# Routing products spread over TensorE's work, the routing chain moved behind the first inner blocks, and one step of the count blocks moved forward

## The chip, the cores and the metric

One Trainium2 chip, one NeuronCore of it. The metric is the device time of one execution in microseconds (us), the median over several runs. Engines: TensorE (PE), its weight loads (PEld), VectorE (DVE), ScalarE (ACT), GpSimd (POOL), SyncE (SP), which issues the transfers.

## What is computed

A graph network on 3125 nodes of 128 features and 100000 edges, in four blocks, each with a layer norm before it and a residual around it. Two of them matter here.

Block 0 is a gated recurrent network of four layers:

```python
for l in range(NUM_LAYERS):            # 4
    m = x @ weight[l]
    agg = segment_sum(m[src], dst)
    x = gru_cell(agg, x, ...)          # reset, update and new gates, x = (1-z)*n + z*x
```

Block 3 is a mixture of experts of three layers, with hidden size 256, four weak and four strong experts:

```python
for l in range(L):                     # 3
    agg = segment_sum(h[src], dst) / deg
    logits = concat([h, agg]) @ router_W[l] + router_b[l]
    gates = softmax of the two largest logits, zero elsewhere
    weak = relu(agg @ weak_W[l] + weak_b[l])                    # 4 experts
    strong = relu(agg @ strong_W1[l] + b1[l]) @ strong_W2[l] + b2[l]   # 4 experts, inner size 512
    h = h + sigmoid(h @ conf_W[l] + conf_b[l]) * sum_e gates[e] * expert[e]
```

Blocks 1 and 2 (two plain graph convolutions, and one with eight relation types) are not touched.

## The kernel before, in words

**Data.** The edges are turned once into a dense matrix of counts `A`, kept in SBUF in fp8; a segment sum is then a product of the node features with `A`. Nodes lie in 25 tiles of 128 (the last of 53), and the tiles in 7 chunks of 4, 4, 3, 4, 3, 4, 3 tiles, so of 512, 512, 384, 512, 384, 512 and 309 columns. A float32 value is carried as two float16 halves, so each sum takes two products per tile and most others three. PSUM has 8 banks, `bank[0]` to `bank[7]`. Every engine has its own list of instructions, written out by hand, and engines are tied by semaphores.

**The expert block** (`block_experts`, from 1635 us to 3197 us of the span). Per layer, the weights come in ten pieces, and ScalarE (`split_high`, L2317) and VectorE (`split_low`, L2170) turn each into two float16 halves in turn. Four of the pieces are split ahead of the first chunk; six (the fifth is `w1` of expert 2, then the two pieces of weak weights, then three more) are split inside the first chunk, behind `hidden(0, 0)`. Per chunk `ci`, TensorE does:

- `route` (L2431): per tile, products with the router's weights in float32, 9 columns wide, into bank 2. VectorE's `route` then adds the bias (L2193, `e_logits`) and runs a chain of small operations that ends in a wait for ScalarE's exponential (L2343) and in the gates (L2233).
- `hidden(ci, e, blocks)` (L2446): the inner blocks of strong expert `e`, 6 products each, into banks 4 and 5 in turn. Block x waits until ScalarE has taken block x-2 out of its bank (`s_kept`, L2353). VectorE then splits each block into halves (L2249, L2251).
- `edges(ci + 1, ...)` (L2407): the segment sum of the next chunk, in pieces between the rest: bank 0 (`KB - 1` = 1 of 2 halves of the features) behind `hidden(ci, 0)`, bank 1 in four pieces.
- `weak` (L2482): products of the weak experts of one tile; needs their weight pieces.
- `strong(ci, e)` (L2465): per tile, 12 products into bank 6 or 7; VectorE empties it (L2260, L2263). The last one, `strong(ci, 3)`, comes behind `turn(ci + 1)` (L2419), the transposes of the next chunk's nodes, and ahead of `route(ci + 1)`.

In VectorE's and in ScalarE's list `route(ci)` stands ahead of `hidden(ci, 0)`. So ScalarE's exponential, which needs VectorE's chain, is queued ahead of its relu of the first inner block.

**The gated block** (`block_gru`). Layer 0 has its segment sums ready from before, so its chunks hold little beside the gates' products. Per chunk TensorE does `gate_b` (L1051), a few tiles of layer 1's first sum, one step of `sym`, `gate_c` (L1063), `finish` of the chunk before (transposes L832 into bank `BT` = 7), and another step of `sym`. `sym` (class `Symmetric`) adds the matrix of packed counts to its transpose for block 2, in 169 steps of up to four transposes (L929) into bank 6 or 7 in turn, by the parity of the step's number, with one VectorE addition each (L948). Two conditions tie it to bank 7:

```python
n, b0, g = STEPS[self.pe_at]
k, bk = n % R, 6 + self.pe_at % 2
...
def other(bk):
    if bk == BT and made["turned"]:
        pe.wait_ge(g_low, made["turned"])
```

`g_low` comes from VectorE (L1299, in layer 3 L1295) once it has read what `finish` put into bank 7. In layer 0 there are two steps per chunk from chunk 1 on, 12 in all. In layers 1 to 3 there are eight steps per chunk, ahead of the tiles that `AMONG` names with "S" (1, 4, 6, 9, 13, 16, 19, 22), and `finish` comes behind the last tile of a chunk, or at tiles 18 and 22 of the next layer's first chunk. VectorE's list has the same steps at the same places (`dve_step`).

## Time and profile before

| what | value |
|---|---|
| median of 3 runs | 3232.41 us (3229.61 to 3233.78) |
| the profiled execution | 3232.69 us, span 3230.8 us |
| mean granted TensorE clock | 0.971 of full speed |
| TensorE busy | 2968.3 us, 92% of the span |
| VectorE busy | 2186.6 us, 68% |
| ScalarE busy | 909.9 us, 28% |

The span runs from the first to the last instruction. A wait is listed by the engine that sat idle and by what ended the idle time. A timeline lists instructions of the same line in one row where they follow each other. Matmuls overlap, so the duration of a row is a little longer than the distance to the start of the next row; the sums of the prediction go by distances between starts.

### The profile page before, as it was taken

How to read it: one execution, taken by the hardware profiler on the slowest of the kernel's cores; microseconds unless marked ns; L12 is line 12 of the kernel's file. 1: busy time of each engine (PE TensorE's matmuls, PEld its weight loads, DVE VectorE, ACT ScalarE, POOL GpSimd, SP SyncE). 2: the span in 40 equal slices, each digit the busy share in tenths (PEclk: the TensorE clock that was granted, in tenths of full speed). 3: DMA queues.
4: the chain of work that ended last, by engine and by line, in shares of the span. 5: the costliest groups of instructions: out<-in, count | busy, mean ns of one | idle time of the engine just before them, and what ended most of it. 6: DMA issues, size and time to landing. Idle time of an engine off the chain costs nothing. (4 is left out here: it accounts for less than half of the span.)

```text
span 3230.8 us, 47504 instructions
## 1 busy us (share of the span) xinstructions
PE 2968.3 (92%) x18761; PEld 1785.9 (55%) x18761; DVE 2186.6 (68%) x4024; ACT 909.9 (28%) x1695; POOL 16.8 (1%) x23
## 2 busy tenths in 40 slices
PE   2888889999988999999989999989999998999997
PEld 2566446656443545454545665655656664656665
DVE  7999555557227777776657666676666686666676
ACT  3888422124101000000032222233222233222222
POOL 2000000000000000000000000000000000000000
PEclk8999889999999999999989999999999999999999
DMA  5455347765006555544330000020000011000001
GB/s 127 144 155 149 95 151 231 229 222 185 22 6 187 157 169 154 178 142 131 83 105 3 4 3 4 3 82 4 6 4 4 3 33 53 3 4 3 4 3 42
DMA packets 310958, 265.84 MB, mean 82 GB/s; under 512 B 32767, under 2 KB 289409, under 8 KB 308174
## 3 DMA queue, kind: packets, MB, share of 16 engines
q1 hardware_dynamic: 296558, 259.28, 26.3%
q10 hardware_dynamic: 13760, 2.61, 0.4%
q8 instruction: 153, 2.51, 0.3%
q0 software_dynamic: 416, 0.85, 0.1%
q14 instruction: 71, 0.58, 0.1%
HBM read 172.67 MB, written 90.05 MB: 81 GB/s over the span
## 5 line engine op out<-in xcount | busy, mean ns | idle before, releaser
L1871 PE MATMUL psum<-r_wd,r_h 128*128 128x512 fp8e4 (+1 forms) x2600 | 567.1, 374 | 14.0 <-ACT r_h L229 13.6
L2446 PE MATMUL psum<-m_agg,m_weights 128*128 128x512 f16 (+2 forms) x2016 | 422.6, 362 | 33.3 <-ACT m_agg L2353 33.3
L2465 PE MATMUL psum<-m_weights,x_nodes 128*128 128x256 f16 (+1 forms) x3600 | 413.0, 273 | 17.0 <-DVE m_wtmp L2260 15.3
L2407 PE MATMUL psum<-counts,m_h 128*128 128x512 fp8e4 (+2 forms) x2100 | 416.0, 355 | 12.6 <-DVE m_h L2150 12.6
L1871 PEld LDWEIGHTS psum<-r_wd,r_h 128*128 128x128 f16 x2600 | 240.6, 96 | 307.8 <-issue 15.5
L2465 PEld LDWEIGHTS psum<-m_weights,x_nodes 128*128 128x128 f16 (+1 forms) x3600 | 350.3, 98 | 74.4 <-DVE m_wtmp L2260 22.0
L2446 PEld LDWEIGHTS psum<-m_agg,m_weights 128*128 128x128 f16 x2016 | 197.3, 101 | 241.2 <-issue 48.6
L2407 PEld LDWEIGHTS psum<-counts,m_h 128*128 128x128 f16 x2100 | 206.3, 98 | 209.1 <-issue 19.5
L2365 ACT ACTIVATE m_hT<-m_hT,m_g 128x256 f32<-128x256 f32 x300 | 135.3, 500 | 599.4 <-DVE m_hT L2274 599.4
L2353 ACT ACTIVATE m_agg<-psum,x_nodes 128x512 f32<-128x512 f32 (+2 forms) x336 | 236.2, 716 | 144.1 <-PE psum L2446 114.9
L2274 DVE SCALAR_TENSOR_TENSOR m_hT<-psum,x_nodes,m_bias 128x512 f32<-128x512 f32 (+1 forms) x150 | 112.0, 750 | 170.0 <-PE psum L2482 169.8
L2260 DVE SCALAR_TENSOR_TENSOR m_wtmp<-psum,x_nodes,m_bias 128x256 f32<-128x256 f32 (+1 forms) x300 | 144.9, 483 | 119.8 <-PE psum L2465 116.8
L2251 DVE TENSOR_TENSOR x_nodes<-m_agg,x_nodes 128x512 f16<-128x512 f32 (+2 forms) x336 | 209.8, 624 | 11.6
L2482 PE MATMUL psum<-m_weights,m_agg 128*128 128x512 f16 x900 | 206.5, 379 | 0.0
L754 PE MATMUL psum<-oh_c,oh_s 128*128 128x150 f16 x1566 | 156.2, 237 | 48.3 <-ACT counts L789 31.4
L948 DVE TENSOR_TENSOR sym_blocks<-sym_blocks,psum 128x1024 uint16<-128x1024 uint16 (+1 forms) x169 | 110.9, 665 | 96.6 <-PE psum L929 95.0
L754 PEld LDWEIGHTS psum<-oh_c,oh_s 128*128 128x128 f16 x1566 | 112.4, 100 | 111.4 <-issue 68.3
L788 ACT ACTIVATE strip<-psum 128x600 uint16<-128x600 f32 x239 | 162.5, 680 | 35.5 <-PE psum L754 33.7
L1076 PE MATMUL psum<-counts,g_h16b 128*128 128x512 fp8e4 (+2 forms) x700 | 158.4, 357 | 2.7 <-DVE g_h16b L1299 2.7
L2263 DVE SCALAR_TENSOR_TENSOR m_h<-m_wtmp,m_g,m_h 128x256 f32<-128x256 f32 (+1 forms) x300 | 145.3, 484 | 10.7
L2249 DVE CAST x_nodes<-m_agg 128x512 f16<-128x512 f32 (+2 forms) x336 | 131.2, 390 | 17.5 <-ACT m_agg L2353 7.7
L1966 DVE SCALAR_TENSOR_TENSOR x_nodes<-psum,r_dg,x_nodes 128x128 f32<-128x128 f32 (+1 forms) x200 | 70.1, 350 | 106.0 <-PE psum L1823 100.6
(312 smaller groups left out, 3367.2 us busy)
## 6 DMA issues: line engine op xcount, KB each, us to landing
r_wd<-packed_sym SPq DMA_DIRECT2D x120, 640.0 KB, 4.2
packed_counts<-strip SPq DMA_DIRECT2D x21, 1800.0 KB, 7.8
sym_blocks<-packed_counts SPq DMA_DIRECT2D x88, 384.0 KB, 4.5
packed_sym<-sym_blocks SPq DMA_DIRECT2D x84, 384.0 KB, 3.1
w_stage<-in_L_gnn_strong_W SPq DMA_DIRECT2D x12, 1024.0 KB, 6.5
m_weights<-in_L_gnn_strong_W SPq DMA_DIRECT2D x21, 512.0 KB, 4.9
x_parked<-x_nodes SPq DMA_DIRECT2D x2, 1600.0 KB, 5.9
x_nodes<-x_parked SPq DMA_DIRECT2D x2, 1600.0 KB, 6.3
```

The lines of the kernel that those rows point to most:

```text
L754: m = pe.matmul(psum[:, unit_at(u, w):unit_at(u, w) + UC], oh_s[q][:, k, :, v], oh_c[q][:, k, :, v], start=True, stop=True)
L788: act.activation(typed_home, typed, ACT.Copy, scale=0.5).then_inc(kept_a, 1)
L1076: m = pe.matmul(bank[bk][:, 0:cw], h16[l % 2][:, part, i, :], A[:, i, c_:c_ + cw], start=(i == 0 and part == 0), stop=(i == NT - 1 and par ...
L1871: m = pe.matmul(bank[pair[b]][:, 0:2 * cw], h16[:, part, p0 + i, :], f_[:, 2 * b:2 * b + 2, :], start=(p0 + i == 0 and part == 0), stop=(p ...
L2251: vec.tensor_tensor(s_[:, BANK:BANK + cw], wide32, s_[:, 0:cw], ALU.subtract).then_inc(s_split, 1)
L2260: vec.scalar_tensor_tensor(tmp[k % 2][0:r_, :], bank[6 + k % 2][0:r_, 0:H], k_strong[0:r_], bcast[0:r_, ge * H:(ge + 1) * H], ALU.mult, AL ...
L2263: vec.scalar_tensor_tensor(h2[0:r_, i, :], tmp[k % 2][0:r_, :], gates[ci % 2][0:r_, k, ge:ge + 1], h2[0:r_, i, :], ALU.mult, ALU.add).then ...
L2353: act.activation(agg[:, hh % 2, 0:cw], bank[4 + hh % 2][:, 0:cw], ACT.Relu, bias=b1s[:, e * FB + f:e * FB + f + 1], scale=k_hidden).then_i ...
L2407: m = pe.matmul(bank[kb][:, 0:cw], h16[:, part, i, kb * P:(kb + 1) * P], A[:, i, c_:c_ + cw], start=(i == 0 and part == 0), stop=(i == NT ...
L2446: m = pe.matmul(bank[4 + hh % 2][:, 0:cw], w_[:, i, kb, f * P:(f + 1) * P], agg16[:, j, kb, 0:cw], start=(x_ == 0), stop=(x_ == len(todo) ...
L2465: m = pe.matmul(bank[b_][0:r_, 0:H], s_[:, pa[0] * BANK + k * P:pa[0] * BANK + k * P + r_], w_[:, pa[1], f, :], start=(f == 0 and pa == PA ...
L2482: m = pe.matmul(bank[2 + pr % 2][0:r_, :], agg16[:, pa[0], kb, k * P:k * P + r_], w_[:, pa[1], kb, :], start=(y_ == 0), stop=(y_ == len(to ...
```

## The change

Three things are done.

1. In the gated block, one step of `sym` is put behind the last segment sum ahead of layer 0's chunk 1, on TensorE and on VectorE. The number of steps stays 169.
2. On TensorE, the routing products of chunk `ci + 1` are issued tile by tile among the tiles of `strong(ci, 3)`: the first behind its second tile. Those of the first chunk of a layer are issued among the first 12 tiles of `edges(1, [0])`, three tiles and one routing tile in turn, so that 13 tiles of that sum are left behind `hidden(0, 0)`.
3. On VectorE, the bias addition (`logits`) stays ahead of `hidden(ci, 0)`, and the rest of the chain (`route`) goes behind it, as does ScalarE's exponential. In the last chunk both stay ahead.

```diff
--- before.py
+++ after.py
@@ -1123,6 +1123,8 @@
                 pe.wait_ge(gate_high, 1)
                 pe.wait_ge(steps.handle, mark["gate_low"])
                 sum_chunk(0, EARLY + 1, gates_of=0)
+
+                sym.pe_step(other)
                 for ci in range(1, NCH):
                     gate_b(0, ci)
                     for i, _ in tiles_of(CH[ci - 2]) if ci >= 2 else ():
@@ -1352,6 +1354,7 @@
                     if ci == 0:
                         state(0, ci)
                         gate_a(0, EARLY + 1)
+                        sym.dve_step()
                     else:
                         finish(0, ci - 1)
                         sym.dve_step()
@@ -2183,15 +2186,19 @@
                         vec.scalar_tensor_tensor(agg16[:, 1, :, 0:cw], agg[:, :, 0:cw], sc[:, 1:2], agg16[:, 0, :, 0:cw], ALU.mult,
                                                  ALU.subtract).then_inc(e_mean_low, 1)
 
+                    def logits(ci):
+                        n = l * NCH + ci
+                        R_, _, n_ = chunk_rows(CH[ci])
+                        vec.wait_ge(mrw_in, MRW_IN)
+                        vec.wait_ge(e_routed, n + 1)
+                        vec.tensor_tensor(lg[0:R_, 0:n_, :], bank[2][0:R_, 0:n_ * (NE + 1)].rearrange("p (t e) -> p t e", e=NE + 1),
+                                          rb[0:R_, l, None, :].to_broadcast([R_, n_, NE + 1]), ALU.add).then_inc(e_logits, 1)
+
                     def route(ci):
                         n = l * NCH + ci
                         R_, _, n_ = chunk_rows(CH[ci])
+                        l_ = lg[0:R_, 0:n_, 0:NE]
                         vec.wait_ge(prio_made, 1)
-                        vec.wait_ge(mrw_in, MRW_IN)
-                        vec.wait_ge(e_routed, n + 1)
-                        l_ = lg[0:R_, 0:n_, 0:NE]
-                        vec.tensor_tensor(lg[0:R_, 0:n_, :], bank[2][0:R_, 0:n_ * (NE + 1)].rearrange("p (t e) -> p t e", e=NE + 1),
-                                          rb[0:R_, l, None, :].to_broadcast([R_, n_, NE + 1]), ALU.add).then_inc(e_logits, 1)
                         vec.wait_ge(e_logits, n + 1)
                         o1, o2, l2, e_ = (t_[0:R_, 0:n_, :] for t_ in rt)
                         S1 = [sm[0:R_, i_, 0:n_] for i_ in range(10)]
@@ -2285,8 +2292,12 @@
                     for ci in range(NCH):
                         more = ci + 1 < NCH
                         ts = tiles_of(CH[ci])
-                        route(ci)
+                        logits(ci)
+                        if not more:
+                            route(ci)
                         hidden(ci, 0, range(FB))
+                        if more:
+                            route(ci)
                         if ci == 0:
                             for k in range(FIRST, NPC):
                                 split_low(k)
@@ -2371,8 +2382,12 @@
                     act.wait_ge(steps.handle, mark["h_bias", l])
                     for ci in range(NCH):
                         ts = tiles_of(CH[ci])
-                        route(ci)
+
+                        if ci == NCH - 1:
+                            route(ci)
                         hidden(ci, 0, range(FB))
+                        if ci < NCH - 1:
+                            route(ci)
                         if ci == 0:
                             for k in range(FIRST, NPC):
                                 split_high(k)
@@ -2419,18 +2434,21 @@
                                 m = pe.transpose(bank[2 + kb][:, k * P:(k + 1) * P], h2[:, i, kb * P:(kb + 1) * P], ident[:])
                             m.then_inc(h_turned, 1)
 
-                    def route(ci):
+                    def route_tile(ci, k):
+
                         n = l * NCH + ci
-                        pe.wait_ge(e_mean, KB * (n + 1))
-                        pe.wait_ge(h_kept, KB * (n + 1))
-                        pe.wait_ge(mrw_in, MRW_IN)
-                        for i, k in tiles_of(CH[ci]):
-                            r_ = rows_of(i)
-                            for kk in range(2 * KB):
-                                lhs = (hT if kk < KB else agg)[:, kk % KB, k * P:k * P + r_]
-                                m = pe.matmul(bank[2][0:r_, k * (NE + 1):(k + 1) * (NE + 1)], lhs, rw[:, l, kk, :],
-                                              start=(kk == 0), stop=(kk == 2 * KB - 1))
-                        m.then_inc(e_routed, 1)
+                        ts = tiles_of(CH[ci])
+                        r_ = rows_of(ts[k][0])
+                        if k == 0:
+                            pe.wait_ge(e_mean, KB * (n + 1))
+                            pe.wait_ge(h_kept, KB * (n + 1))
+                            pe.wait_ge(mrw_in, MRW_IN)
+                        for kk in range(2 * KB):
+                            lhs = (hT if kk < KB else agg)[:, kk % KB, k * P:k * P + r_]
+                            m = pe.matmul(bank[2][0:r_, k * (NE + 1):(k + 1) * (NE + 1)], lhs, rw[:, l, kk, :],
+                                          start=(kk == 0), stop=(kk == 2 * KB - 1))
+                        if k == len(ts) - 1:
+                            m.then_inc(e_routed, 1)
 
                     def hidden(ci, e, blocks):
                         cw = CH[ci][1]
@@ -2447,10 +2465,10 @@
                                               start=(x_ == 0), stop=(x_ == len(todo) - 1))
                             m.then_inc(s_hidden, 1)
 
-                    def strong(ci, e):
+                    def strong(ci, e, tiles=None):
                         w_ = pair_of(PNO[("w2", e)], FB)
                         pe.wait_ge(w_low, l * NPC + PNO[("w2", e)] + 1)
-                        for i, k in tiles_of(CH[ci]):
+                        for i, k in tiles_of(CH[ci]) if tiles is None else tiles:
                             r_ = rows_of(i)
                             b_ = 6 + k % 2
                             if b_ in freed_at:
@@ -2485,13 +2503,17 @@
 
                     edges(0)
                     turn(0)
+                    ROUTE_IN = 12
+                    per = ROUTE_IN // len(tiles_of(CH[0]))
+                    for i, k in tiles_of(CH[0]):
+                        edges(1, [0], range(k * per, (k + 1) * per))
+                        route_tile(0, k)
                     for ci in range(NCH):
                         more = ci + 1 < NCH
                         ts = tiles_of(CH[ci])
-                        route(ci)
                         hidden(ci, 0, range(FB))
                         if more:
-                            edges(ci + 1, range(KB - 1))
+                            edges(ci + 1, range(KB - 1), range(0 if ci else ROUTE_IN, NT))
                         weak(ci, ts[0:1])
                         for e in range(1, NSG):
                             hidden(ci, e, range(HALF))
@@ -2503,7 +2525,13 @@
                         if more:
                             edges(ci + 1, [KB - 1], CUTS_E[-1])
                             turn(ci + 1)
-                        strong(ci, NSG - 1)
+                            next_ = len(tiles_of(CH[ci + 1]))
+                            for k in range(max(len(ts), next_ + 1)):
+                                strong(ci, NSG - 1, ts[k:k + 1])
+                                if 0 < k <= next_:
+                                    route_tile(ci + 1, k - 1)
+                        else:
+                            strong(ci, NSG - 1)
 
                 for l in range(NLAY):
                     dve_layer(l)
```

## Rows read from the trace of the kernel before

**Rows 1.** The page, busy time of the engines (share of the span) and instructions.

```profile
PE 2968.3 (92%) x18761; PEld 1785.9 (55%) x18761; DVE 2186.6 (68%) x4024; ACT 909.9 (28%) x1695; POOL 16.8 (1%) x23
```

**Rows 2.** TensorE's waits, 1680 to 3200 us: us in total, times, longest.

```profile
PE psum L2446 <- ACT m_agg L2353: 32.3, 32, 2.1
PE psum L2465 <- DVE m_wtmp L2260: 15.3, 21, 1.4
```

**Rows 3.** Timeline of TensorE, expert layer 0: start us, us, engine, line [idle before].

```profile
1748.09 2.79 PE L2465 MATMUL psum<-m_weights,x_nodes 128*128 128x256 f16 x24 [0.87 <-DVE m_wtmp L2260]
...
1754.21 2.75 PE L2446 MATMUL psum<-m_agg,m_weights 128*128 128x512 f16 x12
1758.39 2.76 PE L2446 MATMUL psum<-m_agg,m_weights 128*128 128x512 f16 x12 [1.43 <-ACT m_agg L2353]
1760.99 8.29 PE L2407 MATMUL psum<-counts,m_h 128*128 128x384 fp8e4 x50
...
1832.01 2.12 PE L2446 MATMUL psum<-m_agg,m_weights 128*128 128x384 f16 x12 [1.86 <-ACT m_agg L2353]
```

**Rows 4.** Timeline of all engines, expert layer 1, its first chunk.

```profile
2185.02 1.04 PE L2419 MATMUL psum<-ident,m_h 128*128 128x128 f32 x8
...
2191.27 7.81 PE L2446 MATMUL psum<-m_agg,m_weights 128*128 128x512 f16 x24
2191.55 0.20 DVE L2193 TENSOR_TENSOR x_nodes<-psum,m_rb 128x36 f32<-128x36 f32 x1 [2.46 <-PE psum L2431]
...
2194.57 0.21 ACT L2343 ACTIVATE x_nodes<-x_nodes 128x8 f32<-128x8 f32 x1 [6.80 <-DVE x_nodes L2219]
...
2195.98 0.19 DVE L2233 TENSOR_TENSOR m_g<-m_rt,m_rt 128x32 f32<-128x32 f32 x1
...
2198.91 10.96 PE L2407 MATMUL psum<-counts,m_h 128*128 128x512 fp8e4 x50
...
2200.39 0.69 DVE L2251 TENSOR_TENSOR x_nodes<-m_agg,x_nodes 128x512 f16<-128x512 f32 x1
...
2201.00 1.28 DVE L2170 SCALAR_TENSOR_TENSOR m_weights<-m_weights,m_wmax 128x1024 f16<-128x1024 f32 x1
...
2209.71 2.75 PE L2482 MATMUL psum<-m_weights,m_agg 128*128 128x512 f16 x12
...
2213.80 1.28 DVE L2170 SCALAR_TENSOR_TENSOR m_weights<-x_nodes,m_wmax,m_weights 128x1024 f16<-128x1024 f32 x1 [1.28 <-ACT m_weights L2317]
...
2220.97 2.79 PE L2465 MATMUL psum<-m_weights,x_nodes 128*128 128x256 f16 x24 [1.14 <-DVE m_wtmp L2260]
```

**Rows 5.** Timeline of TensorE, start of expert layer 1.

```profile
2161.38 23.80 PE L2407 MATMUL psum<-counts,m_h 128*128 128x512 fp8e4 x100 [4.20 <-DVE m_h L2150]
```

**Rows 6.** Waits, all engines, gated layer 0, 377 to 450 us.

```profile
PE psum L929 <- DVE g_h16b L1299: 19.4, 6, 3.4
```

**Rows 7.** Timeline of all engines, gated layer 0.

```profile
404.93 0.75 DVE L1270 SCALAR_TENSOR_TENSOR g_t<-psum,g_sc,g_r 128x512 f32<-128x512 f32 x1 [0.77 <-ACT g_r L1170]
...
408.13 0.56 DVE L1299 SCALAR_TENSOR_TENSOR g_h16b<-psum,g_h16b 128x384 f16<-128x384 f32 x1 [1.74 <-ACT g_h16b L1184]
...
408.84 1.09 PE L929 MATMUL psum<-ident,sym_blocks 128*128 128x128 f32 x4 [3.14 <-DVE g_h16b L1299]
...
410.57 0.69 DVE L1280 TENSOR_TENSOR g_t<-g_ht,g_n 128x512 f32<-128x512 f32 x1
...
412.62 0.69 DVE L1262 SCALAR_TENSOR_TENSOR g_hn<-g_ht,g_hn 128x512 f16<-128x512 f32 x1
...
416.69 0.62 DVE L1270 SCALAR_TENSOR_TENSOR g_t<-psum,g_sc,g_r 128x384 f32<-128x384 f32 x1 [0.50 <-ACT g_r L1170]
```

**Rows 8.** Timeline, gated layer 1 (two rows) and gated layer 3.

```profile
483.22 0.60 PE L929 MATMUL psum<-ident,sym_blocks 128*128 128x128 f32 x4
...
483.69 0.69 DVE L1299 SCALAR_TENSOR_TENSOR g_h<-psum,g_h 128x512 f16<-128x512 f32 x1 [1.47 <-ACT g_h L1184]
...
729.71 0.69 DVE L1295 TENSOR_TENSOR x_nodes<-x_nodes,psum 128x512 f32<-128x512 f32 x1 [0.77 <-PE psum L832]
```

## The prediction

> **What bounds the kernel now.** I read the page first: TensorE is busy for 92% of the span [rows 1], so the kernel gets faster only where TensorE idles or runs at its lower clock. The waits come next, by stage. In the expert block TensorE loses 32.3 us to ScalarE's relu of inner blocks and 15.3 us to VectorE's emptying of the strong experts' banks [rows 2]. The timeline shows where [rows 3]. Behind the routing products two inner blocks run, TensorE then idles for 1.43 us (512 columns) or 1.86 us (384), and two more follow. The reason is ScalarE's order: the exponential stands ahead of the relu, and it comes 3.0 us after VectorE's bias addition (L2193 to L2343) [rows 4]. The other loss is 0.87 us ahead of the third tile of the last strong expert [rows 3].
>
> In gated layer 0 the waits show six stops of TensorE, 19.4 us together, at a count step [rows 6]. That is the step behind `finish`: it writes bank 7, and VectorE must first have read the transposes there. The timeline shows one of 3.14 us, and a chunk takes 11.76 us from one L1270 to the next [rows 7].
>
> **Part 1, routing chain behind the inner blocks, chunks 1 to 5.** Each layer has three such chunks of 512 columns and two of 384. For 512, the four blocks took 1760.99 - 1754.21 = 6.78 us; twice the second pair (1760.99 - 1758.39 = 2.60) is 5.20, so 1.58 us go. For 384 I take the idle time and 0.14 us for the pipeline's refill, 2.0 us. Sum 9 x 1.58 + 6 x 2.0 = 26.2 us. What could come next: the second pair then waits for the relu alone, which is shorter than the two blocks between, and the split by VectorE (about 1.1 us per block) keeps up with a block of 1.30 us. VectorE ends its splits 2.17 us after TensorE's last inner block (2198.91 to 2201.08) [rows 4]; then come the chain and the gates (2195.98 + 0.19 - 2191.75 = 4.4 us), so the gates are there 6.6 us after the blocks. TensorE has the next chunk's sum there, 50 products, 10.80 us for 512 columns [rows 4] and 8.29 for 384 [rows 3], before the weak products. So the chain is hidden in chunks 1 to 5. The last chunk keeps its order and its waits.
>
> **Part 2, routing products between strong tiles.** One routing tile costs 0.87 us (1748.09 to 1754.21 is 6.12 us, less 2.63 us for two strong tiles, over four). It is the same work elsewhere; what it brings is that it fills the 0.87 us ahead of the third tile. Of the 15.3 us, I leave some 3.8 us (three first chunks, 1.14 in the row shown [rows 4]) and 2.0 us (last chunks), and take 9.5 us. The end of the products, and so `e_routed`, stays where it is.
>
> **Part 3, the first chunk of each layer.** Here the move speaks against the change, because the six weight splits stand behind the chain on both engines. In layer 1 [rows 4]: the transposes end at 2185.02 + 0.88 = 2185.9. With 24 products of the sum (5.2 us, 0.216 each) and 3.5 us of routing, routing ends at 2194.6 instead of 2191.3; inner blocks end at 2199.8, VectorE's splits at 2202.0, the gates at 2206.4. The first of the six splits then starts at 2206.4 instead of 2201.0, the last ends at 2220.5 instead of 2215.1 (2.56 us each). TensorE finished the rest of the sum at 2199.8 + 26 x 0.216 = 2205.4 and needs the second split for its weak products: it stands from 2205.4 to about 2210. It then stops again at the third tile of the first strong expert, which VectorE releases 5.9 us after its last split (2215.1 to 2220.97), so at 2226.4. That point moves by +5.4 us, though TensorE had 4.3 us less to do before it. Three layers: +16.2 us. The idle time of 0.79 us ahead of routing and the slow routing products there lie before that point and bring nothing.
>
> What the stops do to the clock: the stop of 4.20 us at the layer's start was followed by 100 products in 23.80 us [rows 5], where 100 at full clock take 21.6. A stop of about this size comes right before the point above. I take 1.5 us a layer, between 0 and 2.2: +4.5 us. The Trainium skill, "TensorE: Matmul & The Clock Gate", section "HAM oscillation", describes kernels in which each wait between groups of matmuls throttles the engine again, so that the next group starts cold and the wait costs more than its idle time; the row agrees (2.2 us on top of 4.20). Taken in full this would be 2.1 us more.
>
> Expert block: -26.2 - 9.5 + 16.2 + 4.5 = -15.0 us.
>
> **Part 4, one count step ahead of layer 0's chunk 1.** The step itself is two transposes, some 0.2 us, and pushes the next to four: +0.44 us ahead of chunk 1's gates, hidden by nothing. It takes as much from layer 3, which is full: -0.44. SyncE's loads run four pieces ahead and its list is unchanged, so I cost the queue at nothing; a piece that came late would be one stop, for whose size I take the 3.14 us of the stops there [rows 7] as the far end. What counts is parity: every later step changes its bank.
>
> In layer 0 the step behind `finish` now writes bank 6 and needn't wait; the other one writes bank 7, behind `gate_b` and sum tiles. The wait left is VectorE's own chain [rows 7]: L1270 to L1299 3.20 us, two operations and the step without TensorE's delay 1.8, three state operations 2.05 (410.57 to 412.62), next chunk's half 0.7, step 0.7: 8.45 us instead of 11.76. TensorE's work for a chunk at full clock is about 7 us, so VectorE bounds. Five such distances give -16.5 us. The waits' sum of 19.4 is the upper bound; if the clock falls in the remaining gaps of 1 to 1.5 us, 11 is the lower. I take 15.0 net of the 0.44.
>
> In layers 1 to 3 parity works the other way. `finish` is followed by one tile and then by the step at tile 1, so far in bank 6; now it is bank 7 and waits for L1299. In the rows the step started at 483.22 and L1299 ends at 483.69 + 0.69 = 484.38 [rows 8]: 1.16 us. This comes four times a layer, 8 x 1.16 = 9.3 in layers 1 and 2. In layer 3 only one addition stands behind the transposes; it ends 0.9 us after them [rows 8], less 0.43 for the tile: 0.5 us, 4 times, 2.0. At two layer crossings the step at tile 22 becomes free, 0.55 us each (estimate, the step's own work): -1.1. With -0.44: +9.8 us.
>
> Gated block: -15.0 + 9.8 = -5.2 us.
>
> **Sum.** -20.2 us on the profiled execution's 3232.69 is 3212.5 us. The median is 3232.41, 0.3 us below, so 3212.
>
> **The rivals.**
>
> - *The first chunk's delay is absorbed.* If TensorE's stops there only replace what it waits for now and cost nothing net, 20.7 us less: 3191 us. For it: the old stops lie in the same place. Against: VectorE and ScalarE work in turn there without a gap, and both get the chain later. Chance 0.10.
> - *The waits of the inner blocks move instead of going.* With the exponential away, the third block waits for VectorE, which comes from the reduction of the chunk's maximum and the bias addition, or the clock stays low behind the first chunk. If half of the 26.2 us come back: 3212.5 + 13.1 = 3225.6 us. For it: behind the last strong tile VectorE has some 2.4 us to do (an estimate from its list: two additions, one reduction). Against: TensorE needs 1.3 us for block 0, and up to 1.7 us for routing tiles before it. Chance 0.14.
> - *Slower: bank 7 in layers 1 to 3.* If the new stop behind each of the 12 `finish` is as long as in layer 0, 3.14 us [rows 7], it costs 37.7 us instead of 11.3: 3212.5 + 26.4 = 3239 us. It decides from (20.2 + 11.3) / 12 = 2.6 us a stop. For it: same engines, same semaphore. Against: the rows of layers 1 and 3 show ScalarE and VectorE free at that time [rows 8]. Chance 0.06.
> - The change moves no product out of TensorE's work; if neither wait were bound to what is moved, the time would stay at 3232. The rows name both engines, so 0.02.
>
> The forecast has 0.68.
>
> **How the numbers follow.** The forecast's own bounds: best case layer 0 -19.4 and no clock loss, 3203; worst case layer 0 -11, first chunk with 2.2 us of clock each and one more stop of the 4.9 us kind not covered, 3226. The range 3196 to 3228 reaches toward the first rival and holds most of the second. This kernel's measurement can tell about 0.2%, 6.5 us, from no change. Faster by more: the forecast whole, the first rival, and half of the second, 0.84. Within 0.2%: 0.10. Slower: 0.06.
>
> **What would show it.** Right: the 32.3 us wait falls to under 12 us; L2465's wait keeps only first and last chunks; a new wait of TensorE for L2170's weight halves, some 5 us, three times; the 19.4 us in layer 0 gone, and 12 new waits at L929 of 0.5 to 1.3 us in layers 1 to 3. Wrong: a third tile of the first strong expert that is not late; 384-column chunks that still stop in `hidden(ci, 0)`; L1270 in layer 0 still 11 us apart; stops of over 2.6 us behind `finish`.

## The result, and the profile after

The changed kernel takes 3216.85 us (median of 5 runs, 3213.69 to 3218.61); the kernel before, run beside it, 3230.16 us (5 runs, 3227.57 to 3233.78). The medians differ by 13.3 us, where 20.2 were forecast. The ratio on record is 0.9953, interval 0.9943 to 0.9964 (the two medians divided give 0.9959, inside it). The time lies in the range (3196 to 3228) and is faster by more than 0.2%.

The page after, busy times of the engines; it answers to [rows 1]. The span is 3216.3 us (before 3230.8), the mean granted clock 0.975 (before 0.971).

```profile
PE 2951.0 (92%) x18761; PEld 1780.5 (55%) x18761; DVE 2189.7 (68%) x4024; ACT 914.5 (28%) x1695; POOL 18.1 (1%) x23
```

TensorE runs the same 18761 instructions and is busy 17.3 us less (2968.3 to 2951.0). So part of the gain is not idle time at all: the same products ran at a higher granted clock. The forecast has the clock only as a cost and no term for such a gain.

The waits of TensorE after, 1636 to 3190 us (the first two rows are the same for 1680 to 3200 us); they answer to [rows 2] (L2446 is now L2464, L2465 is L2483).

```profile
PE psum L2464 <- ACT m_agg L2364: 21.7, 21, 3.8
PE psum L2483 <- DVE m_wtmp L2267: 16.4, 15, 4.9
PE psum L2500 <- DVE m_weights L2173: 13.7, 3, 4.6
```

The third row is the forecast new wait for the weight halves: three times, 4.6 us each. The first fell from 32.3 to 21.7 us, not to under 12, and its longest grew from 2.1 to 3.8 us. Of the 32.3, only 15.9 us stood at the third block of chunks 1 to 5 (11 stops in 15 chunks); all of it is gone, and 5.1 us came in the three last chunks. That growth is the wait that the forecast had set at nothing, below.

For a table by stage I took the distance between fixed points of the timeline in both profiled executions: in gated layer 0 the first and the seventh L1270 (L1272 after) that starts a chunk; the first product of the expert block; in each expert layer the start of each chunk's transposes (L2419, after L2434).

| stretch (us) | before | after | difference | forecast |
|---|---|---|---|---|
| up to the first L1270 | 373.11 | 376.11 | +3.0 | 0 |
| gated layer 0, first to seventh | 65.15 | 47.11 | -18.0 | -15.0 |
| from there to the expert block (layers 1 to 3) | 1202.3 | 1213.6 | +11.3 | +9.8 |
| experts, first chunk of a layer | 80.1, 78.6, 78.7 | 85.5, 85.3, 85.3 | +18.7 | +20.7 |
| experts, chunks 1 to 5 of a layer | 359.2, 359.2, 360.9 | 347.9, 346.3, 347.9 | -37.1 | -35.7 |
| experts, last chunk of a layer | 82.3, 81.7, 53.6 | 84.9, 84.2, 56.4 | +8.0 | 0 |

(The last entry of the last row is shorter since no layer follows.) Every forecast term has its sign, and one term that was set at nothing is +8.0 us. The first row is the stretch in which the counts are made, which the change does not touch; over all thirteen profiles of this case it takes 371.5 to 376.3 us, so its +3.0 is not put down to the change. The other rows together are -17.1 us; the span fell by 14.5.

**Gated layer 0 and 1 after**, timelines; they answer to [rows 7] and [rows 8].

```profile
400.19 0.75 DVE L1272 SCALAR_TENSOR_TENSOR g_t<-psum,g_sc,g_r 128x512 f32<-128x512 f32 x1
...
400.80 0.60 PE L929 MATMUL psum<-ident,sym_blocks 128*128 128x128 f32 x4
...
404.01 1.47 PE L1076 MATMUL psum<-counts,g_h16b 128*128 128x512 fp8e4 x6 [1.15 <-DVE g_h16b L1301]
...
408.19 0.61 DVE L1272 SCALAR_TENSOR_TENSOR g_t<-psum,g_sc,g_r 128x384 f32<-128x384 f32 x1
...
467.70 0.60 PE L832 MATMUL psum<-ident,g_ht 128*128 128x128 f32 x4
...
469.04 0.69 DVE L1301 SCALAR_TENSOR_TENSOR g_h<-psum,g_h 128x512 f16<-128x512 f32 x1 [1.42 <-ACT g_h L1186]
...
469.88 0.63 PE L929 MATMUL psum<-ident,sym_blocks 128*128 128x128 f32 x4 [1.14 <-DVE g_h L1301]
```

In layer 0 the count step (L929) no longer waits, its four transposes take 0.60 us instead of 1.09, and a chunk takes 408.19 - 400.19 = 8.00 us instead of 11.76. In layer 1 the step behind the gated transposes now waits 1.14 us for L1301; 1.16 were worked out from [rows 8]. The waits of TensorE at L929, gated layers after, 375 to 800 us:

```profile
PE psum L929 <- DVE g_h L1301: 4.6, 4, 1.3
PE psum L929 <- DVE g_h16b L1301: 4.6, 4, 1.3
PE psum L929 <- DVE x_nodes L1297: 2.6, 4, 1.0
```

The 19.4 us of [rows 6] are gone, and 12 new waits of 11.8 us together have come, of 0.4 to 1.3 us each. In layer 0 a part of the wait has moved on: TensorE now waits for L1301 at L1076 (the row at 404.01), 9.0 us in 7 stops from 377 to 450 us, where before it waited there once for 1.2. These are the remaining gaps of 1 to 1.5 us that the forecast named: VectorE's list bounds these chunks.

**Expert layer 1, first chunk after**, timeline; it answers to [rows 4].

```profile
2178.06 1.04 PE L2434 MATMUL psum<-ident,m_h 128*128 128x128 f32 x8
...
2187.34 5.34 PE L2464 MATMUL psum<-m_agg,m_weights 128*128 128x512 f16 x24
2187.60 0.20 DVE L2194 TENSOR_TENSOR x_nodes<-psum,m_rb 128x36 f32<-128x36 f32 x1 [5.46 <-PE psum L2448]
...
2198.75 0.19 DVE L2240 TENSOR_TENSOR m_g<-m_rt,m_rt 128x32 f32<-128x32 f32 x1
...
2198.97 1.28 DVE L2173 SCALAR_TENSOR_TENSOR m_weights<-m_weights,m_wmax 128x1024 f16<-128x1024 f32 x1
...
2202.88 4.35 PE L2500 MATMUL psum<-m_weights,m_agg 128*128 128x512 f16 x12 [4.58 <-DVE m_weights L2173]
...
2211.78 1.29 DVE L2173 SCALAR_TENSOR_TENSOR m_weights<-x_nodes,m_wmax,m_weights 128x1024 f16<-128x1024 f32 x1 [1.28 <-ACT m_weights L2328]
...
2218.95 4.46 PE L2483 MATMUL psum<-m_weights,x_nodes 128*128 128x256 f16 x24 [4.36 <-DVE m_wtmp L2267]
```

The gates (L2240) now end behind the inner blocks, and the first split starts 2198.97 - 2178.06 = 20.9 us behind the transposes, 4.9 later than before (2201.00 - 2185.02 = 16.0). TensorE stops for 4.58 us at the weak products and for 4.36 at the third strong tile. That tile starts 2218.95 - 2178.06 = 40.9 us behind the transposes instead of 35.9 (2220.97 - 2185.02): 4.9 us later, where 5.4 were forecast. Both groups behind the stops are slow: 12 products in 4.35 us instead of 2.75, 24 in 4.46 instead of 2.79.

### The profile page after: what moved, and what is told of

Read it like the earlier page. It is cut to its first block and busy times, and to the rows that moved or that the text cites. A ratio compares the mean times of both kernels' runs of the same rounds, so it can differ in the third digit from the quotient of the medians.

```text
span 3216.3 us, 47575 instructions
## 1 busy us (share of the span) xinstructions
PE 2951.0 (92%) x18761; PEld 1780.5 (55%) x18761; DVE 2189.7 (68%) x4024; ACT 914.5 (28%) x1695; POOL 18.1 (1%) x23
## 5 line engine op out<-in xcount | busy, mean ns | idle before, releaser
L2483 PE MATMUL psum<-m_weights,x_nodes 128*128 128x256 f16 (+1 forms) x3600 | 419.7, 275 | 18.0 <-DVE m_wtmp L2267 16.4
L2464 PE MATMUL psum<-m_agg,m_weights 128*128 128x512 f16 (+2 forms) x2016 | 410.3, 356 | 21.7 <-ACT m_agg L2364 21.7
L2483 PEld LDWEIGHTS psum<-m_weights,x_nodes 128*128 128x128 f16 (+1 forms) x3600 | 353.7, 99 | 73.3 <-DVE m_wtmp L2267 16.5
L2464 PEld LDWEIGHTS psum<-m_agg,m_weights 128*128 128x128 f16 x2016 | 194.9, 99 | 218.8 <-issue 32.7
L2500 PE MATMUL psum<-m_weights,m_agg 128*128 128x512 f16 x900 | 212.2, 386 | 13.7 <-DVE m_weights L2173 13.7
L1076 PE MATMUL psum<-counts,g_h16b 128*128 128x512 fp8e4 (+2 forms) x700 | 157.4, 356 | 11.3 <-DVE g_h16b L1301 11.3
L2256 DVE CAST x_nodes<-m_agg 128x512 f16<-128x512 f32 (+2 forms) x336 | 131.5, 391 | 46.6 <-ACT m_agg L2364 32.3
L2270 DVE SCALAR_TENSOR_TENSOR m_h<-m_wtmp,m_g,m_h 128x256 f32<-128x256 f32 (+1 forms) x300 | 145.4, 485 | 10.7
L2500 PEld LDWEIGHTS psum<-m_weights,m_agg 128*128 128x128 f16 x900 | 88.9, 100 | 112.9 <-DVE m_weights L2173 17.4
```

What stands on the lines that cost most here:

```text
L1076: m = pe.matmul(bank[bk][:, 0:cw], h16[l % 2][:, part, i, :], A[:, i, c_:c_ + cw], start=(i == 0 and part == 0), stop=(i == NT - 1 and par ...
L2270: vec.scalar_tensor_tensor(h2[0:r_, i, :], tmp[k % 2][0:r_, :], gates[ci % 2][0:r_, k, ge:ge + 1], h2[0:r_, i, :], ALU.mult, ALU.add).then ...
L2464: m = pe.matmul(bank[4 + hh % 2][:, 0:cw], w_[:, i, kb, f * P:(f + 1) * P], agg16[:, j, kb, 0:cw], start=(x_ == 0), stop=(x_ == len(todo) ...
L2483: m = pe.matmul(bank[b_][0:r_, 0:H], s_[:, pa[0] * BANK + k * P:pa[0] * BANK + k * P + r_], w_[:, pa[1], f, :], start=(f == 0 and pa == PA ...
L2500: m = pe.matmul(bank[2 + pr % 2][0:r_, :], agg16[:, pa[0], kb, k * P:k * P + r_], w_[:, pa[1], kb, :], start=(y_ == 0), stop=(y_ == len(to ...
```

## The experiments

Each was timed against the kernel before on its own chip: 3229.84 us (first four), 3228.89 (the next four), 3229.56 (the last three). The intervals reach 0.0009 to 0.0016 to each side, 3 to 5 us; a difference between two experiments, or between one and the kernel after, is known no better.

| label | edit | median us | ratio to before (interval) |
|---|---|---|---|
| e1_gated_only | before, with the count step | 3224.74 | 0.9982 (0.9973 to 0.9991) |
| e2_experts_only | after, without the count step | 3223.69 | 0.9976 (0.9967 to 0.9985) |
| e3_banks_only | before, banks 6 and 7 swapped | 3225.24 | 0.9985 (0.9976 to 0.9994) |
| e4_banks_back | after, swapped back from step 13 | 3207.23 | 0.9932 (0.9918 to 0.9945) |
| e5_first_order | after, first chunk's chain ahead again | 3215.47 | 0.9953 (0.9938 to 0.9969) |
| e6_first_as_before | after, first chunk wholly as before | 3200.66 | 0.9914 (0.9901 to 0.9928) |
| e7_last_in_a_row | after, last chunk's routing in a row | 3207.47 | 0.9931 (0.9918 to 0.9945) |
| e9_chain_ahead | after, chain ahead in every chunk | 3252.34 | 1.0069 (1.0054 to 1.0084) |
| e8_all_in_a_row | after, routing of chunks 1 to 6 in a row | 3240.73 | 1.0034 (1.0022 to 1.0046) |
| e10_all_three | e4, e6 and e7 together | 3185.78 | 0.9860 (0.9845 to 0.9875) |
| e11_last_split | e10, last chunk's chain amid its blocks | 3189.30 | 0.9876 (0.9860 to 0.9891) |

### The two halves alone: e1 and e2

e1 adds the count step to the kernel before, and nothing else; e2 takes it out of the kernel after.

```diff
                 sum_chunk(0, EARLY + 1, gates_of=0)
+
+                sym.pe_step(other)
...
                         gate_a(0, EARLY + 1)
+                        sym.dve_step()
```

> The kernel before with the count step ahead of layer 0's chunk 1 alone. The theory: it carries what the profile after shows for the gated block, some 6 to 7 us, so about 3224 us; the six stops at the step behind finish in layer 0 are gone and layers 1 to 3 have 12 new ones of 0.5 to 1.3 us. Rival: the gated block's shorter time came from a run that happened to be quick there; then it is within 1 us of the kernel before.

> The changed kernel without the count step, so the expert block's two parts alone. The theory: the two parts add up; the expert block is 10.5 us shorter than before (from the first segment sum to the first transposes of the output: 1546.6 us against 1557.1), the kernel about 3219.5 us. Rival: the parts share something (the clock, transfers), and the sum of this gain and the count step's is off from 13.3 us by over 3.

Measured: -5.1 us for e1, -6.2 for e2, together 11.3 of the 13.3. e1 came as expected; e2 is 4.2 us slower than expected (3219.5). Both gains are smaller than their stages in the profiles of before and after say (6.7 and 10.5 us). For e2, its own profile shows it: the expert block takes 1550.8 us, 6.3 less than before (1557.1), and not the 1546.6 of the kernel after, whose expert code is the same. One code thus differs by 4.3 us over this block between two executions. For e1 the reason shows in e2, whose gated code is that of before. Windows over the start of gated layer 0 (stretch, length, busy PE, PEld, DVE, ACT, POOL, granted clock, DMA share, GB/s), first before, then e2, then e1:

```profile
377.00:418.00 41.00, 30.62 (x135) 16.21 (x133) 21.94 (x36) 12.84 (x23) 0.00 (x0) 0.79 0.26 76
```

```profile
376.00:417.00 41.00, 28.06 (x147) 15.98 (x146) 25.18 (x43) 14.82 (x26) 0.00 (x0) 0.92 0.38 123
```

```profile
377.00:418.00 41.00, 33.97 (x195) 19.25 (x194) 29.32 (x52) 17.87 (x31) 0.00 (x0) 1.00 0.48 151
```

The same code took 65.15 us in the profile of before (clock 0.79) and 57.76 in that of e2 (0.92). The stops at the count step are alike in both (19.4 and 19.3 us), so it is not they that differ: the layer with its stops varies with the clock that it is granted, and the profile of before has the longer of the two. With the step it took 47.1 us in e1 and in after, at 1.00.

### Place or parity: e3 and e4

e3 is the kernel before with no step moved; only the bank of every count step is the other one. e4 is the kernel after, with the banks as before from step 13 on.

```diff
+    def sym_bank(at):
+        return 6 + (at + 1) % 2
...
-            k, bk = n % R, 6 + self.pe_at % 2
+            k, bk = n % R, sym_bank(self.pe_at)
...
-            k, bk = n % R, 6 + self.dve_at % 2
+            k, bk = n % R, sym_bank(self.dve_at)
```

In e4 the function returns `6 + at % 2 if at < 13 else 6 + (at + 1) % 2`. The waits on the step that last used a bank follow it.

> The kernel before, no step moved, but every count step takes the other bank of 6 and 7. The theory (the bank decides, not the step's place): the same as with the count step moved, within 1 us, about 3224 us, layer 0's chunks 7.6 to 8.7 us apart instead of 11.6. Rival (the place decides: more work ahead of the gates): layer 0 stays as before, and the time is 3230 us or over it by the stops of the later layers, up to 3240.

> The changed kernel, with the banks of the count steps swapped back from layer 1 on (step 13 and later), so that the step at tile 1 takes bank 6 again. The theory: the 12 stops behind finish in layers 1 to 3 (4.6, 4.6 and 2.6 us in the profile after) go, layer 0 keeps its gain: 10 to 12 us less than the changed kernel, about 3206 us. Rival: TensorE then stops at the next tile's product for the same halves of the state, and less than 3 us is won.

e3 gives what e1 gives (3225.24 and 3224.74), with the same waits of TensorE, 375 to 800 us (its line numbers are 6 higher than those of the kernel before):

```profile
PE psum L935 <- DVE g_h L1305: 4.6, 4, 1.3
PE psum L935 <- DVE g_h16b L1305: 4.6, 4, 1.3
PE psum L935 <- DVE x_nodes L1301: 2.6, 4, 1.0
```

So the gain of the gated block comes from the parity and not from the earlier step. e4 is 9.6 us faster than the kernel after, and its layers 1 to 3 are back at 1203.0 us (1202.3 before, 1213.6 after). Of the 12 stops behind `finish` none is left; its waits at the count step for VectorE's reading of bank 7, both elsewhere:

```profile
PE psum L935 <- DVE g_h16b L1307: 1.3, 1, 1.3
PE psum L935 <- DVE g_h L1307: 1.3, 1, 1.3
```

### The first chunk: e5 and e6

e5 puts only the chain and the exponential ahead of the inner blocks in the first chunk; e6 does this and also leaves its routing products in a row.

```diff
-                        if not more:
+                        if ci == 0 or not more:
                             route(ci)
                         hidden(ci, 0, range(FB))
-                        if more:
+                        if ci and more:
                             route(ci)
...
-                        if ci == NCH - 1:
+                        if ci in (0, NCH - 1):
                             route(ci)
                         hidden(ci, 0, range(FB))
-                        if ci < NCH - 1:
+                        if 0 < ci < NCH - 1:
                             route(ci)
```

and for e6 in addition

```diff
-                    ROUTE_IN = 12
-                    per = ROUTE_IN // len(tiles_of(CH[0]))
+                    ROUTE_IN = 0
                     for i, k in tiles_of(CH[0]):
-                        edges(1, [0], range(k * per, (k + 1) * per))
                         route_tile(0, k)
```

> The changed kernel, but in the first chunk of each layer the routing chain and the exponential stand ahead of the inner blocks again; the routing products stay among the sum's tiles. The theory (VectorE's and ScalarE's six weight splits are what the first chunk waits for): the splits start 18.8 us after the transposes instead of 20.9, so the first chunk takes 83.2 us instead of 85.3, the kernel 6 us less, 3211 us. Rival (the stops are made by late weight halves alone, and the order doesn't matter since all of it is done one after the other): no change, 3217.

> The changed kernel with the first chunk of each layer wholly as before: routing products straight behind the transposes, chain ahead of the inner blocks. The theory: the first chunk takes about 78 us instead of 85.3, three times, so 20 to 22 us less: about 3196 us. Rival (the first chunk's loss is absorbed or comes from something else, such as the clock after the layer's start): under 6 us less.

e6 is 16.2 us faster than the kernel after (20 to 22 were expected), and its expert block is shorter by as much (1546.56 to 1530.34). The first chunk takes 79.0, 78.6 and 78.6 us again, 19.8 us less in all; 3.6 us of that came back in stretches whose code is the same. e5 brings almost nothing in the median (3215.47 against 3216.85), so neither the expected 6 us nor clearly nothing. Its first chunks take 85.0, 82.9 and 82.8 us: in two layers of three the expected 83.2 is there, 5.4 us in all, and half of it is lost again in the last chunks (86.7 and 85.0 us instead of 84.9 and 84.2), whose code is the same. Waits of TensorE in e5 and its third strong tile in layer 1:

```profile
PE psum L2483 <- DVE m_wtmp L2267: 16.9, 15, 5.0
...
PE psum L2500 <- DVE m_weights L2173: 4.7, 6, 1.1
```

```profile
2215.93 4.46 PE L2483 MATMUL psum<-m_weights,x_nodes 128*128 128x256 f16 x24 [4.68 <-DVE m_wtmp L2267]
```

The wait for the weight halves fell from 13.7 to 4.7 us, but the stop at the third tile stayed (4.68 us) and with it the slow products. The splits start 2195.95 - 2177.43 = 18.5 us behind the transposes, between the 16.0 of before and the 20.9 of the kernel after. The logits are late by the 24 products of the sum that stand among the routing tiles, so the splits are late by that, and TensorE has those products no longer to put behind. The order of the chain and the place of the routing products must both go back; in e6 the wait at L2483 is 6.6 us instead of 16.4.

### The last chunk: e7 and e11

```diff
-                            for k in range(max(len(ts), next_ + 1)):
+                            if ci + 2 == NCH:
+                                strong(ci, NSG - 1)
+                                for k in range(next_):
+                                    route_tile(ci + 1, k)
+                            for k in range(max(len(ts), next_ + 1)) if ci + 2 < NCH else ():
```

> The changed kernel with the routing products of the last chunk alone in a row behind the last strong tile, as before. The last chunk keeps its chain ahead of its inner blocks, and there TensorE waited 2.1 us before and 3.8 us after. The theory: the routing tiles put ahead of the last strong tiles make VectorE's last additions and its maximum, and so the chain, 1.7 us later against TensorE; in a row the wait is 2.1 us again, 2 to 2.7 us less in each layer, about 3209 to 3211 us. Rival (the wait grew because the products end earlier, nothing lost): no change, 3217.

e7 is 9.4 us faster than the kernel after (6 to 8 were expected; the last chunks in its profile are 6.8 us shorter). The stop at the third inner block of the last chunk is the reason. Timeline of the kernel after, last chunk of expert layer 0:

```profile
2093.19 0.82 PE L2434 MATMUL psum<-ident,m_h 128*128 128x128 f32 x6
...
2101.29 1.75 PE L2464 MATMUL psum<-m_agg,m_weights 128*128 128x309 f16 x12
...
2102.02 1.22 DVE L2314 TENSOR_REDUCE m_hmax<-m_h 128x1 f32<-128x1024 f32 x1
2103.15 0.17 DVE L2194 TENSOR_TENSOR x_nodes<-psum,m_rb 128x27 f32<-128x27 f32 x1
...
2106.84 3.03 PE L2464 MATMUL psum<-m_agg,m_weights 128*128 128x309 f16 x12 [3.79 <-ACT m_agg L2364]
```

and of the kernel before, at the same place:

```profile
2102.72 0.82 PE L2419 MATMUL psum<-ident,m_h 128*128 128x128 f32 x6
...
2110.11 1.22 DVE L2303 TENSOR_REDUCE m_hmax<-m_h 128x1 f32<-128x1024 f32 x1
...
2111.07 1.75 PE L2446 MATMUL psum<-m_agg,m_weights 128*128 128x309 f16 x12
2111.28 0.19 DVE L2193 TENSOR_TENSOR x_nodes<-psum,m_rb 128x27 f32<-128x27 f32 x1
...
2114.91 1.75 PE L2446 MATMUL psum<-m_agg,m_weights 128*128 128x309 f16 x12 [2.08 <-ACT m_agg L2353]
```

Behind the transposes the reduction starts after 8.83 us instead of 7.39: VectorE gets the last strong tile later, since routing tiles stand ahead of it. The bias addition on the logits stands behind the reduction and is late by 1.4 us, and so is everything up to the relu. TensorE finishes its routing products no later (2101.29 - 2093.19 = 8.10 us against 2111.07 - 2102.72 = 8.35). So it waits 3.79 us instead of 2.08, and the 12 products behind take 3.03 us instead of 1.75. In e7 the wait's longest is 2.2 us again.

e11 goes on from e10 (below): in the last chunk two inner blocks, the chain, two blocks.

```diff
-                        if ci == 0 or not more:
+                        if ci == 0:
                             route(ci)
-                        hidden(ci, 0, range(FB))
-                        if ci and more:
+                        hidden(ci, 0, range(FB if more else HALF))
+                        if ci:
                             route(ci)
+                        if not more:
+                            hidden(ci, 0, range(HALF, FB))
```

(and the same on ScalarE)

> As the kernel with all three repairs, but in the last chunk VectorE and ScalarE take the first two inner blocks ahead of the chain and the other two behind it. The theory: TensorE's wait of 2.1 us at the third block goes and a shorter one (under 1 us) comes at the next expert's first block, 1 us less per layer, 3 us in all against the kernel with all three repairs. Rival (VectorE's list of the last chunk is the bound, whatever its order): within 1 us of it.

It brought nothing (3189.30 against 3185.78, where 3 us less were expected, or within 1 us by the rival). The waits of TensorE, first e10, then e11:

```profile
PE psum L2470 <- ACT m_agg L2370: 17.9, 22, 2.2
...
PE psum L2489 <- DVE m_wtmp L2273: 6.6, 15, 1.7
```

```profile
PE psum L2493 <- DVE m_wtmp L2273: 15.2, 15, 3.1
PE psum L2474 <- ACT m_agg L2372: 13.5, 22, 1.2
```

4.4 us left the wait for the relu and 8.6 us came to that for the strong tiles: moving the chain within VectorE's list moves the stop. That this list is what bounds the last chunk fits this, but no run made the list shorter.

### Which half of the expert change does it: e8 and e9

e8 keeps the chain behind the inner blocks and puts the routing products of chunks 1 to 6 in a row again, as they were. e9 keeps them spread and puts the chain ahead of the blocks in all chunks.

```diff
-                            for k in range(max(len(ts), next_ + 1)):
-                                strong(ci, NSG - 1, ts[k:k + 1])
-                                if 0 < k <= next_:
-                                    route_tile(ci + 1, k - 1)
+                            strong(ci, NSG - 1)
+                            for k in range(next_):
+                                route_tile(ci + 1, k)
```

```diff
-                        if not more:
-                            route(ci)
+                        route(ci)
                         hidden(ci, 0, range(FB))
-                        if more:
-                            route(ci)
```

> The changed kernel with the routing products of chunks 1 to 6 in a row behind the last strong tile, as before; chains stay behind the inner blocks in chunks 1 to 5, the first chunk stays as changed. The theory: the waits for a strong bank of 0.87 and 0.29 us come back (8 us in all, less what is left of them now, 0.17 us each, so +6.5), the last chunk gets 7.5 to 9 us better as in the run with the last chunk alone: between 3213 and 3216 us, so spreading the products is worth about 6 us where the chain stands behind. Rival (spreading brings nothing but the last chunk's loss): 3207 us, as with the last chunk alone in a row.

> The changed kernel with the chain and the exponential ahead of the inner blocks in every chunk; the routing products stay spread out. The plain sum (term of 26.2 us comes back, the first chunk gets 6 us better) gives 3237 us. If spreading the products also makes VectorE's chain 1.7 us later against TensorE wherever the chain stands ahead, as theorised for the last chunk, some 22 to 25 us come on top: about 3260 us, with waits of 3 to 3.8 us at the third inner block.

e9 takes 3252.34 us, 15 over the plain sum (3237) and 8 short of the expected 3260, and its wait for the relu (L2458 there) is 60.9 us in 37 waits, the longest 3.8. So the late logits cost there too, though less than expected, and not in every chunk. What fits the rows is how many routing tiles are left behind the last strong tile, since VectorE has that long to empty it. With three left (chunks 3 and 5) TensorE waits 1.5 us at the third inner block, as before (1.4); with two (chunk 1) 2.0 to 2.1 (1.4 before); with one (chunks 2 and 4) 3.3 to 3.6 (1.9 before). Transposes to transposes, layer 1, chunks 1 to 5 take 75.6, 69.0, 74.3, 69.0 and 71.2 us before and 75.1, 71.5, 73.5, 69.8 and 70.4 in e9: chunks 1, 3 and 5 are even a little shorter than before, 2 and 4 longer. Most of what puts e9 above the kernel before lies in the first chunks (+13.0 us in the profiles) and the last (+9.5).

e8 was a surprise, and the most instructive run: at 3240.73 us it is slower than the kernel before, though its waits for the relu are as short as in e7, and some 25 us above what was expected of it. TensorE in e8, chunk 3 of expert layer 0:

```profile
1891.16 1.48 PE L2483 MATMUL psum<-m_weights,x_nodes 128*128 128x256 f16 x12 [0.87 <-DVE m_wtmp L2267]
...
1895.53 0.59 PE L2448 MATMUL psum<-m_rw,m_agg 128*128 128x9 f32 x4
1895.97 7.03 PE L2464 MATMUL psum<-m_agg,m_weights 128*128 128x512 f16 x24
1902.84 8.29 PE L2422 MATMUL psum<-counts,m_h 128*128 128x384 fp8e4 x50
```

and in the kernel after:

```profile
1893.16 5.34 PE L2464 MATMUL psum<-m_agg,m_weights 128*128 128x512 f16 x24
1898.34 8.29 PE L2422 MATMUL psum<-counts,m_h 128*128 128x384 fp8e4 x50
```

The four blocks have no gap in either, yet take 6.87 us (1902.84 - 1895.97) in e8 and 5.18 in after. The granted clock in e8, chunk 1, in steps of 2 us (columns as above):

```profile
1752.00:1754.00 2.00, 2.00 (x13) 1.59 (x13) 0.27 (x2) 0.00 (x0) 0.00 (x0) 0.68 0.00 0
1754.00:1756.00 2.00, 2.00 (x6) 0.76 (x5) 0.00 (x0) 0.00 (x0) 0.00 (x0) 0.50 0.02 4
1756.00:1758.00 2.00, 2.00 (x11) 0.84 (x9) 1.07 (x2) 1.29 (x2) 0.00 (x0) 0.96 0.00 0
```

0.50 is the lower level, 1.2 GHz. TensorE was busy throughout these 6 us, and had been since 1746.91, where a stop of 0.87 us ended; then came 24 float16 products and 32 narrow float32 ones (128x9), 3.8 us long, and the clock fell within the last of these. In e8, 10 of the 15 chunks 1 to 5 have a part of their blocks at the half clock; in the kernel after 2 (both a chunk 5, which like chunk 3 has 2.60 us of routing products in a row at the end), in the kernel before 6.

The other profiles make this firmer. In the kernel after, e2, e4, e5, e6, e7, e10 and e11, chunks 1 to 5 have the chain behind the blocks and the products spread, and what still stands in a row just ahead of the blocks is 8 narrow products in chunks 2 and 4, 16 in chunk 1 and 24 in chunks 3 and 5. The blocks had the half clock in 0 of 48, 0 of 24 and 23 of 48 chunks; in e8, behind 24 in a row in 2 of 6 and behind 32 in 8 of 9. The stop of 0.87 us is not needed for it: in e10, chunk 5 of layer 1, the longest idle time in the 8 us ahead was 0.17 us, and the clock still fell to 0.50.

In the kernel before, 4 of the 6 chunks with the half clock have 512 columns, and there it stood in place of the stop for the relu: blocks at full clock and a stop of 1.43 us take 6.78 us from start to start, blocks at half clock without one 6.86 (2281.17 - 2274.31):

```profile
2274.31 7.03 PE L2446 MATMUL psum<-m_agg,m_weights 128*128 128x512 f16 x24
2281.17 1.14 PE L2407 MATMUL psum<-counts,m_h 128*128 128x384 fp8e4 x6
```

So neither edit brings much alone. Chunk 1 of layer 0, transposes to transposes: 75.5 us before, 75.6 with the chain moved alone (e8), 75.3 with the products spread alone (e9), 73.0 with both. Over all 15 chunks, against before: -7.4 us with the chain alone, +4.4 with the spreading alone, -37.1 with both. The 7.4 us are in chunks that kept the full clock, such as chunk 4 (67.0 us in e8, 69.0 before).

Between e8 and e7, which differ only in the spreading in chunks 1 to 5, lie 33 us of the medians; 28 us (1567.75 - 1539.83) of the expert block in the profiles, 29.7 of them in chunks 1 to 5. A chunk that has the full clock in both is 0.6 to 0.8 us longer in e8 (66.98 and 66.36 for chunk 4, 69.53 and 68.72 for chunk 5): some 11 us for 15 chunks, which is what the stops of 0.87 us bring. The other 19 are an estimate of what the half clock costs, in 10 chunks of e8 against 2 of e7; a chunk loses 1.7 us by it, or 3.3 where the clock fell earlier, in the narrow products (three of the ten).

### All repairs together: e10

> All three repairs together: banks swapped back from layer 1 on (-9.6 us in its own run), first chunk as before (-16.2 to -20), last chunk in a row (-9.4). The theory (three separate places): they add up, 3216.9 - 35 to 39 = 3178 to 3182 us. Rival (they share a bound or the clock gives part of it back): over 3187 us.

3185.78 us, ratio 0.986 (0.9845 to 0.9875): 31 us less than the change as made, and 1.4% less than before. The repairs one by one came to 9.6 + 16.2 + 9.4 = 35.2 us; the 4 us between are no more than the noise of the four medians. The profile of e10 shows a difference of this kind all the same: in e10 chunks 3 and 5 of every layer take 73.5 and 70.4 us, their half-clock values, where the kernel after has 71.8 in chunk 3 (six chunks at the half clock against two, 6.7 us), and its last chunks take 84.1 and 83.9 us in layers 0 and 1 where e7, with the same code there, has 81.8 and 82.0. This is the version to keep.

## Why the prediction was right or wrong

- **Part 1, the chain behind the inner blocks.** The rows, and the sum of the two parts (-37.1 against -35.7), were right: blocks that took 6.78 us take 5.18. The reason was half of it. That the four blocks of 6.78 us would take 5.20 holds at the full clock alone, and e8 shows that with the products in a row the clock mostly does not stay there: the chain alone brought 7.4 us in these chunks and not 26.2, and the spreading alone, booked at -9.5, +4.4. The 32.3 us of [rows 2] could have warned too: the term of 26.2 us counts a stop in all 15 chunks 1 to 5, 24.0 us of idle time, but only 15.9 us of it stood there, since 4 of the 15 chunks had the half clock in the stop's place, and "under 12 us" was out of reach. The split of the sum between the parts was wrong; that the sum came out is owed to both edits being made together, which the forecast did not know to matter. [Rows 3] show a chunk at the full clock; the rows of layer 1 at 2274.31 would have warned.
- **Part 2, the products between strong tiles.** "The end of the products, and so `e_routed`, stays where it is" is true for TensorE (8.10 us behind the transposes against 8.35), but it is not what the chain waits for: the logits are read by VectorE behind the last strong tile's additions and the maximum, and the spread delays that tile. Where the chain was moved behind the blocks this costs nothing. The last chunk keeps its chain ahead, and there it costs 2.6 to 2.9 us a layer, 1.7 of wait and the rest in slow products behind it: +8.0 us over three layers by the profiles, 9.4 by the median of e7. So the step that failed is "The last chunk keeps its order and its waits": the order stayed, the wait grew from 2.08 to 3.79 us, since I did not follow the moved products into it. With this term the forecast sum is -12.2, and -13.3 was measured. By blocks it fits as well: the expert block's -15.0 becomes -7.0, and e2 measured -6.2.
- **Part 3, the first chunk.** Right in mechanism and size: the weak products' wait came three times at 4.58 us (some 5 forecast), the third tile stands for 4.4 to 4.9 us. +18.7 us against 20.7. e6 confirms it with 16.2 in the median and 19.8 in its first chunks. The 1.5 us of clock a layer, taken between 0 and 2.2, measured 4.46 - 2.79 = 1.67 us behind the stop at the third tile; in layer 1 this and the 4.94 us by which that tile is late make up the whole 6.6 us of the chunk. This agrees with the Trainium skill, "TensorE: Matmul & The Clock Gate", section on HAM oscillation: the wait costs more than its idle time.
- **Part 4, the count step.** Right in mechanism: parity, as e3 shows with no step moved. Layer 0 brought 18.0 us in the profile (15.0 forecast, 19.4 its bound), layers 1 to 3 cost 11.3 (9.8). In the median of e1 the two come to 5.1 us, where -5.2 was forecast. That this fits so closely is in part luck: layer 0 before took 65.2 us in one profile and 57.8 in another by the clock it got, so its gain was 18.0 or 10.7 us.
- **The rivals.** The slower one, bank 7 at over 2.6 us a stop, fell: the stops are 0.4 to 1.3 us. The absorbed first chunk fell with e6. Of the rival that inner-block waits move, the mechanism is real for one chunk in seven (the last), though not where it was placed, in chunks 1 to 5. Its sentence "behind the last strong tile VectorE has some 2.4 us to do" named the very list that is late there.
- **The sign** rests on gated layer 0 and the chunks 1 to 5 (55.1 us less in the profiles). The parts that the change makes slower (layers 1 to 3, first chunk, last chunk) come to 38.0 us.
- **The sums.** Two do not come out as written: the worst case as listed (4.0 + 2.1 + 4.9 us above 3212.5) gives 3223.5 and not 3226, and the chances for "faster by more" (0.68 + 0.10 + 0.07) give 0.85 and not 0.84. Neither changes the range or the reading.

Left open: why TensorE's clock falls behind 24 narrow float32 products in 23 of 48 chunks and not in all or none, and so why one code takes a few us more in one execution than in another. No run tried a spreading that leaves at most 16 in a row in every chunk, which the tally suggests.

## What to carry to other kernels

When products are spread among others, follow what is delayed in between (here the last strong tile, and VectorE's list behind it), not only the end of the spread products, and do so for the chunks that the change leaves as they were. Here the two effects pull against each other: the fewer routing tiles are left in a row at the end, the better the clock holds, and the later VectorE has the last strong tile. An idle gap that a row shows at the full clock is worth its length only if the work that moves up also runs at the full clock; compare the same place in other layers before the gap is booked. Where two banks alternate by a running number, a step more or less flips every later step, so the flip should be made only where it helps.

## What the runs showed of the hardware

- The granted clock fell to 0.50 while TensorE was busy throughout: behind 32 narrow float32 products in a row, 3.5 to 3.8 us long, the next 24 products took 7.03 us instead of 5.34 (e8, chunk 3 of layer 0). It fell in 8 of 9 chunks with 32 in a row (e8), in 25 of 54 with 24 in a row (2.60 us; eight profiles and e8), and in none of 72 with 8 or 16 in a row, where 12 or more float16 products stood between.
- One code of gated layer 0 took 65.15 us in one execution (clock 0.79) and 57.76 in another (0.92), with six stops of 3.1 to 3.4 us in it in both; without these stops it took 46.9 to 47.1 us in all eleven profiles that have the step or the swapped banks.
